# Moving the first half of a deferred attention epilogue from before the next block's first iteration to its fifth

## What is computed

```python
hi = einsum(Qs, Ks) * SCALE            # the selected 32x32 blocks
attn = exp(hi - max_vals)
hi_out, hi_norm = sums of attn @ V and of attn over the selected blocks
low_attn = exp(low - row_max - 10000 * hi_mask) * 32   # 64x64, block means
num = hi_out * hi_corr + low_out * low_corr
den = hi_norm * hi_corr + low_norm * low_corr + 1e-06
out = num / den
x = x + out + channel_mix
```

## Time and profile before

| what | us |
|---|---|
| median of 2 runs | 5907.39 |
| lowest and highest of them | 5899.59, 5915.20 |
| the profiled execution, whole time | 5903.88 |
| its span on the slowest core (core 4) | 5902.3 |
| spans of the 8 cores | 5867.7 to 5902.3 |
| PE busy in the span | 3148.3 |
| DVE busy | 2487.2 |
| ACT busy | 1708.7 |
| POOL busy | 281.5 |

### The profile page before, as it was taken

How to read it: one execution, slowest core, us unless ns; L and a number is a source line. 1 busy time by engine, 2 the same in 40 slices (tenths; PEclk the granted TensorE clock), 3 DMA queues, 4 the chain that set the end, 5 groups by cost and what they waited for, 6 DMA issues and landing times.

```text
span 5902.3 us, 57186 instructions; the slowest of 8 cores (5867.7 to 5902.3 us)
## 1 busy us (share of the span) xinstructions
PE 3148.3 (53%) x11328; PEld 1115.3 (19%) x11513; DVE 2487.2 (42%) x5263; ACT 1708.7 (29%) x2627; POOL 281.5 (5%) x301
## 2 busy tenths in 40 slices
PE   1121203433233343776776776776777677667676
PEld 0021101111111111122122122122122122122122
DVE  3431213344433321652652652642642643653553
ACT  2200000000000001354354354354245245245245
POOL 0000010000000000000000000000000000000000
PEclk9965557767676776787787688788678678689688
DMA  1244001111121111111011011010110110100101
GB/s 60 64 75 88 3 6 47 45 41 42 37 50 43 46 47 31 20 24 20 17 28 20 17 28 20 17 28 19 19 27 17 21 22 15 28 19 19 22 19 22
DMA packets 516779, 181.70 MB, mean 31 GB/s; under 512 B 494282, under 2 KB 495474, under 8 KB 516274
## 3 DMA queue, kind: packets, MB, share of 16 engines
q1 hardware_dynamic: 482386, 130.46, 9.7%
q0 software_dynamic: 34080, 47.56, 4.4%
HBM read 142.23 MB, written 39.34 MB: 31 GB/s over the span
## 4 chain that ended last, share of the span: by engine, by line
PE 36%; DVE 21%; DMA 17%; ACT 14%; issue 11%; DVEq 1%; ACTq 1%; POOL 0%; SPq 0%; POOLq 0%
PE pS L843 8%; DVE bm L771 8%; PE pO L811 7%; ACT aT L858 7%; PE pA L762 6%; PE pA L992 3%; PE pA L516 3%; DMA fW<-wT_r 3%; PE pA L1053 3%; DMA fW<-wT_k 2%; ACT stage L936 2%; DMA nb<-norm_all 2%; DVE fA L501 2%; DMA fW<-wT_v 2%; DVE bis_ge L409 1%
## 5 line engine op out<-in xcount | busy, mean ns | idle before, releaser
L771 DVE TENSOR_REDUCE bm<-pA 128x16 f32<-128x512 f32 x1728 | 1195.0, 692 | 778.6 <-PE pA L762 639.8
L858 ACT ACTIVATE aT<-pS 128x1024 bf16<-128x1024 f32 x1024 | 1048.7, 1024 | 763.3 <-PE pS L843 718.8
L762 PE MATMUL pA<-ktp,qtp 64*128 64x512 bf16 x1728 | 717.3, 428 | 391.4 <-ACT aT L858 109.8
L811 PE MATMUL pO<-aT,vtm 128*65 128x512 bf16 x2048 | 711.1, 433 | 391.8 <-ACT aT L858 390.8
L843 PE MATMUL pS<-rhsc,lhsc 128*128 128x512 bf16 x1928 | 691.3, 442 | 21.5 <-issue 12.6
L516 PE MATMUL pA<-fA,fW 128*128 128x512 bf16 x1504 | 418.0, 428 | 284.6 <-DMA fW<-wT_r 77.3
L417 PE MATMUL pB<-bis_cnt,ones 128*128 128x32 f32 x116 | 35.2, 397 | 681.7 <-DVE bis_cnt L413 681.7
L811 PEld LDWEIGHTS pO<-aT,vtm 128*65 128x65 bf16 x2048 | 237.2, 124 | 730.7 <-issue 582.7
L762 PEld LDWEIGHTS pA<-ktp,qtp 64*128 64x128 bf16 x1728 | 157.6, 95 | 991.2 <-issue 987.1
L771 DVE TENSOR_REDUCE bm<-pO 128x16 f32<-128x512 f32 x320 | 221.3, 691 | 147.9 <-PE pO L762 116.5
L1053 PE MATMUL pA<-xnT,wsl_v 128*128 128x512 bf16 x496 | 173.5, 511 | 186.2 <-issue 115.2
(11 more groups left out here) (148 smaller groups left out, 2640.8 us busy)
## 6 DMA issues: line engine op xcount, KB each, us to landing
xtile<-x SPq DMA_DIRECT2D x64, 512.0 KB
fW<-wT_r SPq DMA_DIRECT2D x64, 256.0 KB
fW<-wT_k SPq DMA_DIRECT2D x64, 256.0 KB
fW<-wT_v SPq DMA_DIRECT2D x64, 256.0 KB
out<-stage SPq DMA_DIRECT2D x32, 512.0 KB
rhsc<-qtp POOLq DMA_DIRECT2D x32, 256.0 KB, 2.9
lhsc<-ktp POOLq DMA_DIRECT2D x32, 256.0 KB, 2.9
bx<-bsm_dram POOLq DMA_DIRECT2D x32, 256.0 KB, 7.7
```

Of the source, the lines that this page charges most:

```text
L762: e.matmul(pap, qtp[p0:p0 + 64, ts0 + t * 128:ts0 + (t + 1) * 128], ktp[p0:p0 + 64, ts0 + kq * 512:ts0 + (kq + 1) * 512], start=True, stop ...
L771: e.tensor_reduce(bmp[:, kq * 16:(kq + 1) * 16], pap.rearrange("p (k e) -> p k e", e=32), axis=AX.X, op=ALU.max))
L811: e.matmul(pO[0:65, sl * 512:(sl + 1) * 512], vtm[:, (sq * 16 + k) * 130 + hip * 65: (sq * 16 + k) * 130 + hip * 65 + 65], aT[bpar][:, sl ...
L858: e.activation(aT[bpar][:, :], pS[bpar][:, :], AF.Exp, scale=0.125))
```

## The change

Wave 0 is split. Its 8 transposes stay where they were, right after the epilogue's waits. Its DVE pair and its 8 scalings are moved into the function that iteration 4 of the next block calls, ahead of wave 1, which is unchanged in itself. Nothing is added or removed, and no wait is taken out. `emit_wave` gets a parameter for transposes that were already issued:

```diff
-                    def emit_wave(w, gate0=0, gate1=0):
-                        if gate0:
-                            r.wait("tensor", "sAC", gate0)
+                    def emit_wave(w, gate0=0, gate1=0, npe_tr=None):
                         acts = []
-                        for sl8 in range(8):
...
-                        npe_tr = r.cnt["sPE"]
+                        if npe_tr is None:
+                            if gate0:
+                                r.wait("tensor", "sAC", gate0)
+                            for sl8 in range(8):
...
+                            npe_tr = r.cnt["sPE"]
                         r.wait("vector", "sPE", npe_tr)
...
-                    _, acts0 = emit_wave(0)
-
-                    def w1fn(acts0=acts0, b=b, par=par, stg=stg, h=h, sq=sq):
+                    for sl8 in range(8):
+                        r.emit("tensor", lambda e, sl8=sl8: e.transpose(
+                            pA[:, sl8 * 128:sl8 * 128 + 65],
+                            outT[:, sl8 * 128:(sl8 + 1) * 128], id_f[0:65, 0:65]))
+                    npe_tr0 = r.cnt["sPE"]
+
+                    def w1fn(b=b, par=par, stg=stg, h=h, sq=sq, npe_tr0=npe_tr0):
+                        _, acts0 = emit_wave(0, npe_tr=npe_tr0)
                         ndv_rd, acts1 = emit_wave(1, gate0=acts0[3],
                                                   gate1=acts0[7])
```

More of the change, by code:

```diff
@@ L903, in emit_epilogue @@
                                                 state["phA_dv4"][1]))
-                    def emit_wave(w, gate0=0, gate1=0):
-                        if gate0:
-                            r.wait("tensor", "sAC", gate0)
+                    def emit_wave(w, gate0=0, gate1=0, npe_tr=None):
                         acts = []
-                        for sl8 in range(8):
[L910 to L915, removed]
-                        npe_tr = r.cnt["sPE"]
+                        if npe_tr is None:
+                            if gate0:
+                                r.wait("tensor", "sAC", gate0)
+                            for sl8 in range(8):
+                                i = w * 8 + sl8
+                                if gate1 and sl8 == 4:
+                                    r.wait("tensor", "sAC", gate1)
+                                r.emit("tensor", lambda e, i=i, sl8=sl8:
+                                       e.transpose(
+                                           pA[:, sl8 * 128:sl8 * 128 + 65],
+                                           outT[:, i * 128:(i + 1) * 128],
+                                           id_f[0:65, 0:65]))
+                            npe_tr = r.cnt["sPE"]
                         r.wait("vector", "sPE", npe_tr)
```

## The result

The changed kernel took 5852.5 us (median of 11 runs, 5839.5 to 5861.6) against 5900.1 us (10 runs) for the kernel before in the same session: a ratio of 0.992, 95% interval 0.9908 to 0.9931. It is 47.7 us faster, within 2%. The prediction was 5878 us from a forecast gain of 26.7 us, so the gain was 1.8 times the forecast one. The measured time lies half a microsecond inside the lower end of the range (5852 to 5903), near rival C's 5854, but not for rival C's reason.

The account below looks back on a forecast made before the run. Handover stalls between PE, DVE and ACT at block start and iteration 4 were taken as the bound. The terms -83.2 + 1.6 + 62.9 - 8 = -26.7 us gave 5877, median put at 5878 us, range 5852 to 5903.

Parts of the forecast that it names:

- rival C: PE's clock stays up after the block start, the full 31 us gained there: 5854 us; chance 0.14.
- What bounds: Handovers between PE, DVE and ACT stall block start and iteration 4; both stalls lie on the path, one to one.
- Part 1: Block start: without wave 0's eight scalings the first exp comes 3.61 us earlier in 16 places, 3.17 in 8; 83.2 us gained.
- What is late next: Block start: laT, behind the mask build, holds the first exp 0.1 us past its scores in 16 places, 1.6 us lost.
- The rule on the shared ports: Block start: DVE's mask build and POOL's 0.55 us DMA issue need the same ports; whichever comes second waits.
- Rival D: Block start: the mask build waits for POOL's DMA issue, first exp 0.55 us later in 16 places: 5887 us; chance 0.09.
- Part 2: Iteration 4: scalings delay the fifth exp to 8.04 us after exp 3's end, 2.75 or 2.3 us per block; 62.9 lost.
- Part 3: Behind the first emit_av: less PE idling shortens the low-clock stretch, 8 us gained; no change counted after iteration 4.
- A: The move cancels itself: scalings paid in full at iteration 4, 77 us lost there, 5900 us; chance 0.12.
- B: Slower: after iteration 4's longer stall PE's clock stays low, 1.3 us more per block, 5915 us; chance 0.10.
- E: Nothing reaches the end: phase A from iteration 8 on is late anyway and covers both stalls, 5904 us; chance 0.05.
- The signs: Expected in the traces, among others: ACT's wait for denominators falls from 105.8 us to about half.

Follow-up runs that it names:

- e1: Changed kernel with wave 0's DVE pair back at the block's start, only its eight scalings moved to iteration 4; ratio 0.9992 to the kernel before.
- e3: Changed kernel with wave 0's eight scalings issued twice in iteration 4; ratio 1.0062 to the kernel before.
- r_after: The changed kernel run again unaltered, in the session of e5 to e7; ratio 0.9922 to the kernel before.
- e8: Changed kernel with the score pair of iteration 5 issued six times instead of once; ratio 0.9891 to the kernel before.
- e2: Changed kernel with wave 0's DVE pair and scalings in iteration 1, only wave 1 in iteration 4; ratio 0.9988 to the kernel before.
- e5: Changed kernel with emit_prep of blocks 1 and 2 at iteration 7 instead of the block's start; ratio 0.994 to the kernel before.
- e7: Changed kernel with the eighth scaling of wave 0 issued twice in iteration 4; ratio 0.9948 to the kernel before.
- e4: Changed kernel with outT wait and wave 0's transposes and pair in iteration 1, scalings in 2, 3, 5, 6, wave 1's transposes and pair in 4; 5742.7 us, 0.978.
- e6: e4 with emit_prep of blocks 1 and 2 at iteration 7; ratio 0.974 to the kernel before, median 5708.9 us.
- e9: e6 with the score pair issued three times in iterations 3, 4, 6 and 7; 5714.5 us, ratio 0.9696 to the kernel before.

## Why the prediction was right or wrong

The time lies in the range, and the two large terms came out as worked out from the rows. That it lies there at the very edge, with nearly twice the forecast gain, is in part luck: the range's lower end was set for rival C, which did not come, and the effect that took its place was not in the sum.

- *What bounds: right.* Both stalls are on the path one to one (e1 for the start, e3 for iteration 4).
- *Part 1, the start: right in kind, 7% too small.* Forecast -81.6 us with `laT`, measured -87.8. The 16 places with `emit_prep` gave 57.7 us (57.8 without the `laT` term), the 8 without it 30.1 us where I had 25.4. The step that missed is "with scores at the same distance behind the transposes" for these 8: I priced them at the low clock. In the changed kernel 60 of the 64 (8 places on 8 cores) have the full clock for the transposes, and 53 start after 1.5 us; before, 35 of the 64 had it for the transposes.
- *What is late next: the order was wrong, by 1.6 us.* I had `laT` last, 0.1 us behind the scores. In some 104 of 128 places (16 on 8 cores) the scores were last, with `laT` done mostly 0.37 or 0.72 us ahead. The step that missed is the scores' time: mostly they let the exp start 2.35 us after the copy, where I had 2.09 from the earlier trace rows, one of the quicker places. e1 shows how near `laT` was: had the pair stayed, 41 us would have gone.
- *The rule on the shared ports: it is POOL that lost time.* POOL's issue grew from 0.55 to 1.22 us in the rows above, the mask build kept its 1.22 us. That is what the Trainium skill (SBUF — State Buffer, section "Who interferes with whom") says for the one that comes second. Rival D failed because DVE came first, by 0.12 us in that row. Where POOL came first, by 0.33 us, the mask build did not wait for it: 1.23 to 1.24 us instead of 1.22. So there the trace does not show the second one blocked, and rival D's 0.55 us appears nowhere.
- *Part 2, iteration 4: right.* Forecast 2.75 and 2.3 us per block, +62.9; measured 2.52 on average, +60.5. Of the 0.13 us that the row is earlier than E + 8.04, 0.10 is the way from the eighth scaling to the transposes (0.15 us, where I took 0.25) and 0.04 the four transposes and the way to DVE (2958.82 to 2959.43, 0.61 us, where I took 0.65).
- *Part 3, the clock: the place was wrong and the size too small.* I sought 8 us in the stretch behind the first `emit_av`, between exps 0 and 3; there it is 0.3. I counted no change behind iteration 4 and did not look at the clock further on in the block, which put it at nothing without a reason: it is -2.7 us in exps 4 to 8 and -9.7 in 12 to 31. With up to 5 us of part 1 that hang on the clock too, it gave some 13 to 18 us. Why fewer blocks fall to the low clock behind the half-time copy is not settled. The traces narrow it down: low clock in iterations 12 to 31 is 42 to 49 us per core in after, r_after, e1, e3 and e8, which all finish wave 0 in iteration 4, and 75 and 95 us in before and e2, which finish it earlier (e5 and e7 lie between, 59 and 57). e1 is among the low ones although its first exp comes late, so it is not the shorter start that does it.
- *The sum.* The gain was 21 us larger than forecast. Parts 1 and 2 give -27.3 us against a forecast -18.7 (-81.6 + 62.9), 9 us more; part 3's place 8 us less; the exps from 4 on another 13 us that were not in the sum. The last 7 us lie where the change does nothing. They may be scatter between two profiled executions, but in r_after the blocks i = 0 and the stretches between pairs are also 4 us shorter than before, and with one trace of the kernel before it stays open.
- *Rivals.* A is excluded by the two sums, C by exps 0 to 3, D by e5, E by e3. B's mechanism, a longer low stretch behind iteration 4, did not come (exps 4 to 8 take 6.15 us for 6.27).
- *The signs.* The wait for denominators fell to 33.6 us, a third and not half: wave 1's own wait also shrank, from 2.03 us in the earlier trace rows to 1.38, since `emit_av` and half of its transposes are done by the time wave 0's scalings end.

## What to carry to other kernels

When a step with handovers between engines is moved, follow everything that stood behind it in each engine's program, not only the step: here two small DVE operations in front of an unrelated build were worth nearly as much (41 us) as the eight ACT operations (47 us of the 88 gained at the starts). Moving a chain in one piece keeps its stall; issuing each of its steps an iteration ahead of the next (e4, e6) removes it: 2.2 and 2.6% faster than before (e6 by its median 2.9%), against 0.8% for the move. Where PE waits in short stalls, count its low-clock time per stretch, and if it has nothing useful to do, repeating a harmless matmul can pay (18 us in e8, 9 to 13 us in e9).

## What the runs showed of the hardware

- PE's clock costs time far from the place that is changed: 0.27 us per us at the low clock in iterations 12 to 31 (40 cores of five runs), with the low stretches that changed at exps 17 to 20.
- Redundant matmuls made the kernel faster (e8: 0.9922 to 0.9891), by keeping the granted clock up: low clock in exps 4 to 8 fell from 5.1 to 1.7 us per block.
- A DMA issue on POOL takes 1.22 us instead of 0.55 when a mask build of 1.22 us has started on DVE 0.12 us before it, and 0.86 us when it has started 0.47 us before: the issue ends 0.11 to 0.12 us after the mask build in all 14 such places of a core. Issued 0.33 us ahead of the mask build it takes 0.55 us, and the mask build 1.23 to 1.24 (after and r_after).
- Eight scalings of 0.314 us take 3.16 us in a row, 0.407 us from start to start: between two of them lie 0.09 us, and each waits for the one before it.
